# Marking passed rows ahead on GpSimd, and one product of columns moved from ScalarE to VectorE, in the edge sort of a graph kernel

## The reference, cut to what matters

```python
neigh_sum = segment_sum(X[col], row, n); neigh_mean = neigh_sum / denom
H = relu(X @ W_root + neigh_mean @ W_neigh + b)
gg = segment_sum(abs(H[row] - H[col]) ** 2, row, n) / denom
x = x + tanh(gg)
x = x + ffn(layernorm(x))        # router, top 2 of 6 experts, three layers each
```

## Time and profile before

| | |
|---|---|
| median of 3 runs | 2837.13 us (2836.13 to 2838.58) |
| the profiled execution | 2836.03 us, of which the span of the profile is 2834.2 us |
| busy over the span | TensorE 81%, VectorE 70%, ScalarE 31%, GpSimd 72% |
| the column loop | 111.7 to 267.7 us of the span |
| the scatters | first starts at 134.14 us, last at 289.89 us |
| first gather of the first pass | 297.14 us |

### The profile page before, as it was taken

The page is one execution under the profiler, slowest core; times in us unless marked ns, Lnnn a source line. Parts: engine busy times, 40 slices in busy tenths (PEclk is TensorE's granted clock), DMA queues, the critical chain, the costliest instruction groups (busy, mean ns, idle before and its releaser), DMA issues.

```text
span 2834.2 us, 33557 instructions
## 1 busy us (share of the span) xinstructions
PE 2298.4 (81%) x8655; PEld 1296.3 (46%) x8655; DVE 1993.5 (70%) x5304; ACT 872.4 (31%) x2404; POOL 2030.8 (72%) x2021
## 2 busy tenths in 40 slices
PE   6676577777777777777789898888998888899996
PEld 4564444454434444444233333333333333389996
DVE  8997555556655555555578888888888888755456
ACT  7897000001100000000233333333333333355553
POOL 2488777777777777777677777777777766667772
PEclk8598789987677776766899999999999999999998
DMA  4254333334433333333543434344434333332266
GB/s 128 92 143 81 95 106 106 105 106 120 127 105 113 112 113 105 113 112 113 173 119 112 126 118 126 112 124 117 126 112 123 117 93 112 104 102 94 90 190 207
DMA packets 173026, 332.36 MB, mean 117 GB/s; under 512 B 45296, under 2 KB 108636, under 8 KB 172578
## 3 DMA queue, kind: packets, MB, share of 16 engines
q0 software_dynamic: 100224, 249.16, 30.6%
q1 hardware_dynamic: 70306, 78.94, 8.5%
q10 hardware_dynamic: 2304, 2.10, 0.2%
HBM read 279.94 MB, written 40.96 MB: 113 GB/s over the span
## 4 chain that ended last, share of the span: by engine, by line
DVE 28%; PE 24%; POOL 17%; issue 13%; DMA 10%; DVEq 6%; ACT 1%; SPq 0%; POOLq 0%; ACTq 0%
DVE big L1369 19%; PE ps L1320 15%; POOL arena L1276 11%; DMA arena<-xn_table,graph 7%; DVEq L1333 6%; PE ps L2294 5%; POOL edge_list L663 4%; DVE graph L1363 4%; PE ps L2276 3%; DMA arena<-h_table,graph 2%; POOL arena L1803 1%; PE ps L1379 1%; POOL y_by_token L1809 1%; PE ps L2244 1%; DVE big L872 1%
## 5 line engine op out<-in xcount | busy, mean ns | idle before, releaser
L1320 PE MATMUL ps<-arena,graph 128*128 128x258 f32 (+3 forms) x3956 | 1672.7, 593 | 405.9 <-DVE graph L1363 383.8
L1320 PEld LDWEIGHTS ps<-arena,graph 128*128 128x128 f32 (+1 forms) x3956 | 749.9, 223 | 1286.5 <-DVE graph L1363 1025.6
L1369 DVE TENSOR_TENSOR big<-ps,big 128x258 f32 (+1 forms) x1978 | 1100.2, 556 | 112.9 <-PE ps L1320 78.1
L1276 POOL DMA_INDIRECT arena<-h_table,graph x842 | 819.2, 973 | 287.9 <-issue 155.9
L1276 POOL DMA_INDIRECT arena<-xn_table,graph x842 | 799.0, 949 | 261.9 <-issue 191.9
L1363 DVE TENSOR_SCALAR graph<-iota,graph 128x128 f32<-128x128 f32 x1684 | 506.1, 301 | 509.9 <-DMA arena<-xn_table,graph 311.1
L1300 ACT ACTIVATE arena<-arena 128x256 f32<-128x256 f32 x842 | 348.5, 416 | 694.6 <-DMA arena<-h_table,graph 636.0
L1290 ACT ACTIVATE late<-late 128x256 f32<-128x256 f32 x49 | 20.3, 415 | 995.9 <-DVE late L1445 995.9
L1809 POOL DMA_INDIRECT y_by_token<-big,node x106 | 121.0, 1141 | 71.9 <-DVE big L1864 55.1
L663 POOL DMA_INDIRECT edge_list<-big x64 | 138.1, 2158 | 42.9 <-issue 42.3
L1803 POOL DMA_INDIRECT arena<-xn_table,node x106 | 111.8, 1055 | 39.4 <-issue 31.4
(11 more groups left out here) (330 smaller groups left out, 1579.3 us busy)
## 6 DMA issues: line engine op xcount, KB each, us to landing
arena<-xn_table,graph POOLq DMA_INDIRECT x842, 2.8
arena<-h_table,graph POOLq DMA_INDIRECT x842, 2.8
big<-y_by_token SPq DMA_DIRECT2D x48, 256.0 KB, 4.4
big<-graph SPq DMA_DIRECT2D x10, 848.0 KB
h_table<-late SPq DMA_DIRECT2D x49, 128.0 KB, 2.1
late<-h_table SPq DMA_DIRECT2D x49, 128.0 KB, 3.0
xn_table<-late SPq DMA_DIRECT2D x12, 512.0 KB
big<-in_x SPq DMA_DIRECT2D x48, 128.0 KB, 2.6
```

The costliest lines, as they stand in the source:

```text
L1276: e.indirect_dma_start(out=row, out_offset=None, in_=table, in_offset=bass.IndirectOffsetOnAxis(ap=idx[:, t:t + 1], axis=0)).then_inc(s_ro ...
L1320: e.matmul(out_, hot[part, g % HOTS, :], moving, start=True, stop=True).then_inc(s_sum[i], 1)
L1369: e.tensor_tensor(block, ps[a % n_banks][:, 0:width], block, ALU.add)._wait_ge(s_sum[i], a + 1).then_inc(s_add[i], 1)
```

## The change

`BY_ACT` becomes (8, 7): in the 49 steps in which ScalarE has a z row it makes 7 columns, and VectorE's first L1001 grows from 5 to 6 columns.

The buffer `passed` becomes one buffer for each of the 8 chunks, in the part of `big` behind `sorting_end`. VectorE marks chunks 0, 1 and 2, in steps 0, 1 and 2. GpSimd marks chunks 3 to 7 ahead of its scatters: 15 instructions (tensor_scalar, 98 x 512, against a start in float32 from SBUF), which wait for `starts_f`, a small new copy of the starts that VectorE makes just before the loop. TensorE waits for GpSimd's marks in chunks 3 to 7. SP clears the parts of `big` in a rotated order, and the four parts with the new buffers last, behind the last product with them.

```diff
--- before.py
+++ after.py
@@ -93,7 +93,7 @@
     FIRST = 12
     DIGIT = 64
     ROWS_T = TC + 4
-    BY_ACT = 8
+    BY_ACT = (8, 7)
     PR = 8
     HR, XS = 1, 3
     YB, YG, XR = 4, 10, 4
@@ -225,7 +225,6 @@
         dest_f = carve_sort(2 * GG).rearrange("p (h g) -> p h g", h=2)
         dest = carve_sort(CC * GG).bitcast(U32).rearrange("p (c g) -> p c g", c=CC)
         count_h = carve_sort(GG * P // 2).bitcast(F16)
-        passed = carve_sort(3 * GG * P // 2).bitcast(F16).rearrange("p (j r) -> p j r", j=3)
         ends_t = carve_sort(NB2)
         seen = carve_sort((STEP_COLS + UNITS) * NB)[0:STEP_ROWS, :]
         seen_whole = seen[:, 0:STEP_COLS * NB].rearrange("p (r b) -> p r b", b=NB)
@@ -239,6 +238,9 @@
         code_f = carve_sort(TW)
         hot_col = carve_sort(BT * 2 * HI).bitcast(F16).rearrange("p (r t a m) -> p r t a m", r=2, t=BT, a=2)
         sorting_end = at
+        PASSED_EARLY = 3
+        passed_words = 3 * GG * P // 2
+        assert sorting_end + C * passed_words <= NB * W2
         assert codes_at + 2 * NT <= sorting_end
         assert PR == ZR and 2 * KD * D + ZR * D <= 6 * KD * D and Z_AT + NB < TW // BT
         XAT = -(-taken // D)
@@ -266,6 +268,13 @@
 
             bank, place = divmod(k + per - 1, per)
             return ps[bank][:, place * P if bank else 0:][:, 0:min(P, NT - list_blocks[k] * P)]
+        starts_f = big[0:NB2, sorting_end + C * passed_words:sorting_end + C * passed_words + 3 * C].rearrange(
+            "p (j c) -> p j c", j=3)
+
+        def passed(c):
+            at_ = sorting_end + c * passed_words
+            return big[0:NB2, at_:at_ + passed_words].bitcast(F16).rearrange("p (j r) -> p j r", j=3)
+
         by_block = acc.rearrange("p (b w) -> p b w", w=W2)
 
 
@@ -422,6 +431,7 @@
         s_kept = sem("sums_of_units_kept")
         s_jump = sem("row_jumps_and_ends_made")
         s_passed = sem("passed_rows_marked")
+        s_passed_p = sem("passed_rows_marked_by_pool")
         s_jumped = sem("row_jumps_summed")
         s_dest = sem("list_rows_made")
         s_scat = [sem(f"rows_scattered_{i}") for i in range(2)]
@@ -500,6 +510,12 @@
         N_EDGE_DMA = 2 + 2 * (TAIL > 0)
         slot_i, low3, lane_i = bucket_i, other_i, bucket_f.bitcast(I32)
 
+        def by_act(k):
+            return BY_ACT[0 < k - Z_AT <= NB]
+
+        def made_by_act(k):
+            return sum(by_act(j) for j in range(k))
+
         def first_column(k):
 
             q, t = divmod(k, TH // BT)
@@ -554,11 +570,16 @@
         clear_times, clear_over = divmod(NB * W2 - sorting_end, NTR)
         clear_parts = -(-clear_times // CLEAR_BY)
         assert clear_parts < len(z_sets)
+        PASSED_PARTS = -(-(C * passed_words + 3 * C) // (CLEAR_BY * NTR))
+        assert PASSED_PARTS < clear_parts
 
         def sp_clear(e, i):
             if i == 0:
                 e.wait_ge(s_pick, NB)
                 e.dma_start(acc[:, NB * W2 - clear_over:NB * W2], local[:, 0:clear_over]).then_inc(s_cleared, 16)
+            i = (i + PASSED_PARTS) % clear_parts
+            if i == 0:
+                e.wait_ge(s_jumped, C)
             a, z = i * CLEAR_BY, min((i + 1) * CLEAR_BY, clear_times)
             e.dma_start(acc[:, sorting_end + a * NTR:sorting_end + z * NTR].rearrange("p (n w) -> p n w", w=NTR),
                         local.unsqueeze(1).to_broadcast([P, z - a, NTR])).then_inc(s_cleared, 16)
@@ -652,6 +673,12 @@
             e.wait_ge(s_pick, NB)
             e.iota(count_h, [[1, GG * P]], base=0, channel_multiplier=0, **ALL_ONE).then_inc(s_region, 1)
             e.iota(far, [[CODE, MIX]], base=0, channel_multiplier=CODE * ((N - MIX) // P), **ALL_ONE).then_inc(s_region, 1)
+            e.wait_ge(s_jump, 6)
+            e.wait_ge(s_region, 11)
+            for c in range(PASSED_EARLY, C):
+                for j in range(3):
+                    e.tensor_scalar(passed(c)[:, j, :], count_h[0:NB2, :], starts_f[:, j, c:c + 1], None,
+                                    ALU.is_ge).then_inc(s_passed_p, 1)
             for c in range(CC):
                 e.wait_ge(s_dest, min(c, C - 1) + 1)
                 e.wait_ge(s_list, c + 1)
@@ -720,7 +747,7 @@
                 c, t = divmod(k, TH // BT)
                 r = k % 2
                 e.wait_ge(s_hlane, k + 1)
-                e.wait_ge(s_hcola, BY_ACT * (k + 1))
+                e.wait_ge(s_hcola, made_by_act(k + 1))
                 e.wait_ge(s_hcold, 2 * (k + 1))
                 if c >= 2 and t == 0:
                     e.wait_ge(s_list, c - 1)
@@ -768,12 +795,15 @@
             m.then_inc(s_zP, 1)
 
         def pe_rows(e, c):
-            e.wait_ge(s_passed, c + 1)
+            if c < PASSED_EARLY:
+                e.wait_ge(s_passed, c + 1)
+            else:
+                e.wait_ge(s_passed_p, 3 * (c - PASSED_EARLY + 1))
             if c:
                 e.wait_ge(s_dest, c)
             for g in range(GG):
                 for j in range(3):
-                    m = e.matmul(ps[6][:, 4 * g:4 * g + 4], passed[0:NB2, j, g * P:(g + 1) * P],
+                    m = e.matmul(ps[6][:, 4 * g:4 * g + 4], passed(c)[:, j, g * P:(g + 1) * P],
                                  jumps[:, j, c, :, :].rearrange("p h d -> p (h d)"), start=(j == 0), stop=(j == 2))
             m.then_inc(s_jumped, 1)
 
@@ -808,7 +838,7 @@
                 e.wait_ge(s_iscol, k + 1)
                 if k >= 2:
                     e.wait_ge(s_sorted, k - 1)
-                for u in range(BY_ACT):
+                for u in range(by_act(k)):
                     e.activation(hot_col[:, r, u, 0, :], is_col[:, r, u, :], ACT.Copy,
                                  scale=code_f[:, t0 + u:t0 + u + 1]).then_inc(s_hcola, 1)
                 if t == 1 and c:
@@ -982,13 +1012,14 @@
 
             e.tensor_scalar(ends_t[0:NB2, :], ident[0:NB2, 0:NB2], end_of, None, ALU.mult).then_inc(s_jump, 1)
             e.tensor_scalar(at_rank, iota[0:NB, 0:NB], block_t[0:NB, 4:5], None, ALU.is_equal).then_inc(s_jump, 1)
+            e.tensor_copy(starts_f, starts_two[:, :, :, 0]).then_inc(s_jump, 1)
             e.tensor_copy(code_f, high[:, :, 0]).then_inc(s_code, 1)
             e.wait_ge(s_wide, 1)
             for k in range(TW // BT):
                 c, t = divmod(k, TH // BT)
                 r, t0 = k % 2, first_column(k)
                 if k >= 2:
-                    e.wait_ge(s_hcola, BY_ACT * (k - 1))
+                    e.wait_ge(s_hcola, made_by_act(k - 1))
                     e.wait_ge(s_hcold, 2 * (k - 1))
                 e.tensor_tensor(paired(is_col[:, r, :, :]), counted(BT, HI), across(col_of, t0, BT, HI),
                                 ALU.is_equal).then_inc(s_iscol, 1)
@@ -997,11 +1028,11 @@
                 e.tensor_tensor(paired(hot_lane[:, r, :, :]), counted(BT, P), across(lane_of, t0, BT, P),
                                 ALU.is_equal).then_inc(s_hlane, 1)
                 e.wait_ge(s_iscol, k + 1)
-                for i, part, u in ((0, high, BY_ACT), (1, low, 0)):
+                for i, part, u in ((0, high, by_act(k)), (1, low, 0)):
                     e.tensor_tensor(paired(hot_col[:, r, u:BT, i, :]), paired(is_col[:, r, u:BT, :]),
                                     across(part, t0 + u, BT - u, HI), ALU.mult).then_inc(s_hcold, 1)
-                if t == 0 and c < C:
-                    dve_passed(e, c)
+                if k < PASSED_EARLY:
+                    mark_passed(e, k, s_passed)
                 if t == 2 and c:
                     dve_list(e, c - 1)
                 if t == 3 and c < C:
@@ -1109,14 +1140,14 @@
                 e.tensor_tensor(jumps[:, :, :, :, d], a.unsqueeze(3).to_broadcast([NB2, 3, C, 2]), halves,
                                 ALU.mult).then_inc(s_jump, 1)
 
-        def dve_passed(e, c):
+        def mark_passed(e, c, made):
             if c == 0:
                 e.wait_ge(s_region, 11)
                 e.wait_ge(s_jump, 3)
             every = [NB2, 3, GG * P // 2, 2]
-            e.tensor_tensor(passed[0:NB2, :, :].rearrange("p j (r q) -> p j r q", q=2),
+            e.tensor_tensor(passed(c).rearrange("p j (r q) -> p j r q", q=2),
                             count_h[0:NB2, :].rearrange("p (r q) -> p r q", q=2).unsqueeze(1).to_broadcast(every),
-                            starts_two[:, :, c, :].unsqueeze(2).to_broadcast(every), ALU.is_ge).then_inc(s_passed, 1)
+                            starts_two[:, :, c, :].unsqueeze(2).to_broadcast(every), ALU.is_ge).then_inc(made, 1)
 
         def dve_list(e, c):
             e.wait_ge(s_lowp, c + 1)
```

## The result

The changed kernel took 2842.2 us in the median (22 runs), the kernel before 2837.11 us (22 runs beside them); the ratio is 1.0016, with a 95% interval of 1.0010 to 1.0022. So the change costs 3 to 6 us. The forecast was 2845 us, with a range of 2820 to 2857.

A forecast was written before the change was run, and what follows sets the result against it. It took GpSimd's 64 scatters to bound the stage: -13.7 us from recovered scatter slots and +21.6 us from marks holding up VectorE make +7.9 us, added to the median 2837.13 for 2845 us; range 2820 to 2857.

The forecast's parts named there:

- What bounds the stage: From 100 to 310 us, GpSimd's 64 scatters: when the first starts and how long they take; 54.9% of the chain.
- The scatters' gain: Scatter stage if nothing else changed: six lost slots come back, last start 276.2 against 289.89 us, -13.7 us.
- The rule of one scatter a step: Beside VectorE's loop, one scatter each step from step 7 on, 57 by step 63; the rest follow after it.
- The cause given for the long scatters: In the loop's first part, VectorE's marks of 0.87 us make one scatter in three take 5.42 us.
- a shift of phase: Scatters asked for inside L997 get in at its end, those just ahead don't; VectorE's mark shifts the phase.
- The marks' price: GpSimd's 15 marks ahead of the scatters: 1.44 us each, 21.6 us, all taken as lost by VectorE's loop.
- exclude each other: During the marks, VectorE's two-input SBUF instructions and GpSimd's reads take turns; VectorE loses 21.6 us; chance 0.42.
- the order of their turns: Whichever engine goes first during the marks, VectorE's loop ends 21.6 us later.
- 156 for the other reason: First scatter at 156 us under the forecast, in which VectorE stands still for GpSimd's marks; 135 us without exclusion.
- the prediction's own sign: Wrong if VectorE doesn't stand still for the marks, or scatters' pitch in chunks 0 to 7 stays 3.3 us.
- the case that it gave 0.03: Something worse than the listed rivals, such as VectorE starving GpSimd for tens of us; chance 0.03.
- ScalarE's part: In z steps, ScalarE's pitch falls 0.25 us to 2.01, below VectorE's 2.21; worth 1.1 us, nearly cancelled.

The follow-up runs named there:

- vector_ahead: Changed kernel with all eight marks on VectorE, in steps 0 to 7, none on GpSimd; ratio 0.9964 to the kernel before, 0.9969 when repeated.
- marks_again: All eight marks on VectorE ahead of the scatters, plus six repeated VectorE marks in step 0 of chunks 2 to 7; last scatter start 295.66 us.
- split_marks: Kernel before with each VectorE mark from chunk 1 on cut into three thirds, spread over three steps; ratio 1.0011.
- window_each_step: Kernel before with a one-column copy from PSUM on VectorE ending each of the first 32 steps; one execution 2829.61 us, median before 2837.11.
- marks_before_loop: Changed kernel with GpSimd marking chunks 2 to 7 (18 compares) from 94 us on, VectorE chunks 0 and 1 in steps 0 and 4; ratio 0.9968.
- idle_compares: All eight marks on VectorE, plus 15 GpSimd compares into unread buffers ahead of the scatters; one execution 3172.98 us beside 3162.05 before.
- both runs of the parts: Changed kernel with 8 products on ScalarE in every step, ratio 1.0010; kernel before with the moved product alone, ratio 0.9993.

## Why the prediction was right, and where it wasn't

**What bounds the stage** held. Every kernel's end followed its scatters: when the first starts, how many run beside the loop at one a step, how many are left behind it at 1.85 us. In all of them the first gather of the first pass starts 6.9 to 7.7 us behind the last scatter's start.

**The scatters' gain** (13.7 us without the marks' price) held in size. The rule of one scatter a step with a last start at 276.2 us was made for three marks on VectorE. With eight it gives 280.5 us, and `vector_ahead` measured 280.10 and 279.96. In the changed kernel the pitch from 155.21 to 268.24 us is 113.03/50 = 2.26 us, and 13 scatters are left for 24.5 us.

**The cause given for the long scatters was half right.** That VectorE's marks make them is shown by `marks_again` and by `vector_ahead`. That they do so by a shift of phase, and that a scatter asked for inside L997 gets in at its end, failed in `split_marks`, and on the scatter at 139.65 us of the kernel before. What the runs show in its place: a hold lasts until VectorE's next instruction with at most one input in SBUF (for the scatters always one with an input in PSUM), and 1.5 us later the scatter is done (before, `split_marks`, and by construction `window_each_step`). Why a mark, whole or in thirds, makes the scatter behind it miss its turn is left open. Nor is a mark the only way: in `vector_ahead` the scatter at 185.53 us, 45 us behind the last mark, took 2.89 us, and ended 1.50 us behind the start of L1162.

**The marks' price failed as a step, and came out near in the sum.** The prediction had 1.44 us a mark, alone. It is 1.56 us beside the copies from PSUM (`marks_before_loop`), so the 15 would be 23.4 us in place of 21.6. It had the two engines exclude each other, with the whole of it as VectorE's loss, and said that the order of their turns "doesn't matter for the sum". The exclusion is there (compares against counts, 49.05 against 8.02 us). But VectorE hardly lost: in `vector_ahead` its loop ends at 267.9 us with eight marks, so with three 263.5 us; in the changed kernel it ends at 269.5. That is 6.0 us, 0.6 of it a later start of the loop (112.02 against 111.46 us), so 5.4 us, 0.36 a mark, as in `idle_compares`, and not 21.6. GpSimd paid instead, 43.3 us for the marks, and as they stand in front of the scatters in one queue, the first scatter came at 155.2 us, where the prediction had 156 for the other reason. That 155 met 156 is luck, and so is a good part of the sum. By the prediction's own sign, that it is wrong if VectorE doesn't stand still for the marks, its mechanism was wrong. What happened was nearest to the case that it gave 0.03, GpSimd starved by VectorE. The order of turns does matter. With VectorE's loop 16 us shorter than forecast, the scatters' last start was 292.8 us and not the 297.8 of the forecast (276.2 + 21.6); it lay 23.2 us behind the loop's end, where the prediction had some 12.

**The size.** +7.9 us was forecast and +5.1 measured (2.8 to 6.3 by the interval). The stage gives 2.9 us of it, 3.2 by the first gather of the first pass (297.14 and 300.29 us), 3.9 by the first gather of the second (1364.0 and 1367.9 us). All of these lie inside the interval. Whether there is anything beyond isn't known: single executions of the changed kernel spread from 2836.34 to 2846.99 us.

**ScalarE's part** held: the product was costed as near to nothing, and both runs of the parts say so.

**The page of the Trainium skill**, "SBUF — State Buffer", section "Who interferes with whom", says that VectorE with two SBUF inputs contends with a GpSimd instruction that reads SBUF and not with one that only writes; the traces agree, with 49.05 us against 8.02 us for 15. The same page of the Trainium skill says, in the section "SBUF: two separate sides", that of such a pair the one that starts first blocks the other for its whole length. The trace differs: in the changed kernel the first mark was held across four steps' worth of VectorE instructions, 11 us, nearly all of which started behind it, while VectorE waited at most 0.42 us for a mark of 1.56. The section "Who interferes with whom" of the Trainium skill also reports a probe in which tensor_tensor didn't stall GpSimd's DMAs. Here the traces differ again: scatters of 1.55 us took up to 5.48 us beside it, and a copy from PSUM set them free.

## What to carry to other kernels

Before work is given to an idle GpSimd, look at what VectorE does in those microseconds: beside instructions with two inputs in SBUF, a GpSimd instruction that reads SBUF may stand still for as long as they follow each other, and all that is queued behind it on GpSimd waits too; beside reads from PSUM it costs its own time. If GpSimd's DMAs are the bound, a stretch of such VectorE instructions was broken up cheaply here, by moving one of them or by a tiny one that reads PSUM. And when two mechanisms give the same start for the bounding stage, check which engine the profile would show standing still, since the end may differ.

## What the runs showed of the hardware

- GpSimd's compare of 98 x 512 float16: 1.56 us beside VectorE's copies from PSUM, 2.0 to 2.7 us for most of those in the column loop, 10.5 to 14.0 us where it met steps 0 to 3, in which VectorE's first instruction that reads PSUM stands at the end of step 3, and 6.2 to 7.9 us where it was asked for inside a VectorE mark later on.
- GpSimd's count (iota) of the same size: 0.53 us in the same place.
- VectorE's side of the same contention: 0.42 us in two L1032, where a mark got in; 5.4 us for 15 compares, and nothing for 15 counts.
- An indirect DMA with addition on GpSimd: 1.55 us with VectorE idle, 1.6 to 2.19 us beside its loop when it isn't held, about 5.4 us behind a VectorE mark, and 2.79 to 3.54 us behind a mark if each step ends with a copy of one column from PSUM.
